# Quarter products 5 to 7 of a Strassen step in one-bank sums, two of them with 512-column matmuls, and eleven row sums a batch

## The chip, the cores and the metric

The kernel runs on one core of one Trainium2 chip. The metric is device time in microseconds (us) of one execution; lower is better. The core has engines with queues of their own that run side by side and meet at semaphores: TensorE (PE, matmuls into PSUM; its weight loads are shown as PEld), VectorE (DVE), ScalarE (ACT), GpSimd (POOL) and SyncE (SP), whose queue issues nearly all DMAs here. The kernel lays PSUM out as eight banks of 512 float32 columns on 128 partitions: two single ones (`ps_y`) and three tiles of two (`ps_u`, `ps_v`, `ps_p`).

## The reference

For each of 8 batches of 256 rows (H = 1024), an adapter matrix chosen by an index is applied, then a feed-forward layer with a routed low-rank addition, and the input is added:

```python
y = einsum('bsi,boi->bso', x, weight[adapter_ids])        # first product
logits = y @ gate_w.T + expert_bias
top1 = argmax(logits, axis=-1)                            # 4 experts
base = einsum('bth,oh->bto', y, W_up)                     # second product
z = einsum('nh,erh->ner', y, lora_A)                      # rank 8 for each expert
d = einsum('ner,ehr->neh', z, lora_B) * SCALE
out = x + base + sum over e of d[:, e] * one_hot(top1)[:, e]
```

## The kernel before, in words

All matmuls are in fp32r. Each operand is split in a high part (rounded by ScalarE) and a low part (the remainder, by VectorE), and a product is made of three matmuls: high x high, high x low, low x high. TensorE takes, for every batch b, first_product(b): eight output blocks c, each 8 pairs of a 512-column and a 256-column matmul into `ps_y[c % 2]`, which give y. Then comes the second product. Batches 0 and 1 (`b < PLAIN`) do it plainly: 512-column matmuls into one bank for each of four output quarters (`quarter`), with gates and logits apart. Batches 2 to 7 do a Strassen step with seven products (`PARTS = 7`) of quarter matrices: the left sides are A11, S1..S4 and so on, made of y by VectorE; the right sides are B11, T1..T4 and so on, made of W_up once and kept.

In the Strassen step `product(b, n, ps, p, q, ...)` makes product n of left part p and right part q, in four k steps of six matmuls (`quarter_wide`): three operand pairs, each with the 512 output columns cut in two halves of 256. Half h goes to columns 0 to 255 of bank h of a two-bank tile (`ps_u`, `ps_v` or `ps_p`). The room behind the second half, columns from 256 of bank 1, takes 72 or 36 gate and LoRA-A columns in products 1 to 4. Products 5 to 7 have no gate columns. Sums build up in PSUM: products 1, 3, 5 and 7 accumulate in `ps_u`, 2 and 6 in `ps_v`, 4 in `ps_p`, and VectorE adds the state of a tile to the output rows after some of the products (`add_row(b, t, j, ps)`: row block t, column half j, 128x512 elements, one step of `row_step` each). There are eight such sums a Strassen batch. TensorE's products wait for the sums that read a tile they go on writing.

VectorE's order is written out by hand in its `strassen(b)`: the low parts of y (`y_lo_part`), the row sums, the gate sums (`g_kept`, `g_sum`, `zg`), `choose` (expert choice, some 13 small steps that end in `z_parts`), the split of the next batch's input (`x_lo`, four steps), and of its first adapter blocks (`w_lo_part`). TensorE transposes `z_parts` in the middle of product 6 (`transpose_z`), ScalarE copies it back (`z_back`), and four LoRA sums follow (`add_lora`, `add_lora_wide`), one to each output quarter, then product 7. In batch 2 VectorE also splits the second half of T4 between two row sums (`t_lo(T4, 1)`). SyncE's queue stores a batch's rows when `row_step` has reached the last sum of each row block (`store_rows(b, 1, 7)`, `store_rows(b, 0, 8)`), and only then loads further ones.

Of the kernel before, what the change touches and what calls it, by code (L numbers as in the profile page):

```python
# [25 lines left out]
def build(nc, xT, x, ids, w, w_up, gl, lora_b, bias, out):  # L26
# [9 lines left out]
    Q = OC // 2  # L36
# [36 lines left out]
    UNITS_AFTER = range(3, UNITS)  # L73

    parts_before = [4 * min(b, PLAIN) + PARTS * max(b - PLAIN, 0) for b in range(B + 1)]
    rows_before = [4 * min(b, PLAIN) + 8 * max(b - PLAIN, 0) for b in range(B + 1)]
    sums_before = [SUMS * max(b - PLAIN, 0) for b in range(B + 1)]
    gates_before = [5 * max(b - PLAIN, 0) for b in range(B + 1)]
    products_before = [PARTS * max(b - PLAIN, 0) for b in range(B + 1)]
# [1 line left out]
    with ExitStack() as ctx:  # L81
# [70 lines left out]
        def out_cols(ps):  # L152
            return ps[:, :, 0:QUART]
# [85 lines left out]
        def _(sp):  # L239
# [35 lines left out]
            def store_rows(b, t, n):  # L275
                sp.wait_ge(row_step, rows_before[b] + n)
                sp.dma_start(out[b, t * P:(t + 1) * P, :], rows[:, t, :]).then_inc(stored[t], 16)

            def store_part(b, t, j, n):
                sp.wait_ge(row_step, rows_before[b] + n)  # L280
                part = slice(j * HALF, (j + 1) * HALF)
                sp.dma_start(out[b, t * P:(t + 1) * P, part], rows[:, t, part]).then_inc(stored[t], 16)

            def store_batch(b):
                if b < PLAIN:
                    store_rows(b, 0, 2)
                    store_rows(b, 1, 4)
                else:
                    store_rows(b, 1, 7)
                    store_rows(b, 0, 8)  # L290

            def load_blocks(first, stop, i):
                for n in range(first, min(stop, BLOCKS)):
# [23 lines left out]
            for b in range(1, B):  # L317
# [8 lines left out]
                if b + 1 < B:  # L326
                    load_x(b + 1)
                i = load_blocks(first + OC - 1, first + OC, i)
            store_rows(B - 1, 1, 7)
            store_part(B - 1, 0, 0, 7)  # L330
            store_part(B - 1, 0, 1, 8)
            sp.wait_ge(stored[0], (B + 1) * 16)
            sp.wait_ge(stored[1], B * 16)

# [165 lines left out]
        def _(dve):  # L500
            def x_lo(b, q):
                dve.wait_ge(x_hi_ready, b * XQ + q + 1)
                ks = slice(q * XK, (q + 1) * XK)
                dve.tensor_tensor(x_hilo[:, 1, ks, :], x_raw[:, 1, ks, :], x_hilo[:, 0, ks, :].bitcast(F32),  # L504
                                  ALU.subtract).then_inc(x_ready, 1)
# [183 lines left out]
            def strassen(b):  # L689
                dve.wait_ge(y_full_ready, (b + 1) * OC)  # L690
                y_add(S2, A22, S3, ALU.subtract, slice(Q - 1, Q))
                dve.wait_ge(y_sum, sums_before[b] + 3)
                y_lo_part(b, 2, S3)
                y_add(S4, A12, S2, ALU.subtract)
                y_add(S1, A21, A22, ALU.add)
                dve.wait_ge(y_sum, sums_before[b] + 5)
                y_lo_part(b, 3, S2)
                dve.wait_ge(rows_in[0], (b + 1) * 16)
                dve.wait_ge(product_done, products_before[b] + 1)
                dve.tensor_copy(g_kept[:, 0, :], gate_out(ps_u)).then_inc(g_step, 1)  # L700
                add_row(b, 0, 0, out_cols(ps_u))
                y_lo_part(b, 4, A12)
                y_lo_part(b, 5, S1)
                y_lo_part(b, 6, A22)
                y_lo_part(b, 7, S4)
                dve.wait_ge(rows_in[1], (b + 1) * 16)
                dve.wait_ge(product_done, products_before[b] + 2)
                dve.tensor_copy(g_kept[:, 1, :], gate_out(ps_v)).then_inc(g_step, 1)
                add_row(b, 1, 1, out_cols(ps_v))
                if b == PLAIN:  # L710
                    t_lo(T4, 1)
                dve.wait_ge(product_done, products_before[b] + 3)
                dve.wait_ge(g_step, gates_before[b] + 2)
                dve.tensor_tensor(g_sum[:, 1, :], gate_out(ps_u), g_kept[:, 1, :], ALU.add).then_inc(g_step, 1)
                add_row(b, 1, 0, out_cols(ps_u))
                if b + 1 < B:
                    x_lo(b + 1, 0)
                    x_lo(b + 1, 1)
                dve.wait_ge(product_done, products_before[b] + 4)
                dve.tensor_tensor(g_sum[:, 0, :], gate_out(ps_p), g_kept[:, 0, :], ALU.add).then_inc(g_step, 1)  # L720
                dve.wait_ge(g_step, gates_before[b] + 4)
                dve.tensor_tensor(zg[:, :, :], g_sum[:, :, 0:GL], g_sum[:, :, GL:2 * GL], ALU.add).then_inc(g_step, 1)
                dve.wait_ge(g_step, gates_before[b] + 5)
                choose(b, zg[:, :, :])
                if b + 1 < B:
                    x_lo(b + 1, 2)
                    x_lo(b + 1, 3)
                dve.wait_ge(product_done, products_before[b] + 5)
                add_row(b, 1, 1, out_cols(ps_u), after=2)
                for n in splits_after(b):  # L730
                    w_lo_part(n)
                lora_before = PLAIN * 4 + (b - PLAIN) * 4
                dve.wait_ge(out_done, lora_before + 1)
                add_row(b, 1, 1, ps_y[1][:, :].rearrange("p (h n) -> p h n", h=2), after=4)
                dve.wait_ge(out_done, lora_before + 2)
                add_row(b, 0, 0, out_cols(ps_p), after=1)
                dve.wait_ge(out_done, lora_before + 3)
                add_row(b, 1, 0, out_cols(ps_v), after=3)
                dve.wait_ge(out_done, lora_before + 4)
                dve.wait_ge(product_done, products_before[b] + 7)  # L740
                add_row(b, 0, 1, out_cols(ps_u))

            dve.memset(warm_f[:, :], 0.0).then_inc(warm_step, 1)
            dve.wait_ge(warm_step, 1)
# [18 lines left out]
        def _(pe):  # L763
# [117 lines left out]
                        add_lora(b, 1, 0, ps_plain[1, 0])  # L881
                add_lora(b, 1, 1, ps_plain[1, 1])

            def product(b, n, ps, p, q, start, stop=False):
                for k in range(Q):
                    last = quarter_wide(ps, p, q, k, start and k == 0, stop and k == Q - 1, n in (1, 2, 3, 4))
                    if n == 6 and k == 1:
                        transpose_z(b)
                last.then_inc(product_done, 1)

            def strassen(b):
# [17 lines left out]
                pe.wait_ge(y_ready, y_before + 4)  # L909
                product(b, 4, ps_p, A12, B21, True)  # L910
                pe.wait_ge(y_ready, y_before + 5)
                pe.wait_ge(row_step, rows_done + 3)
                product(b, 5, ps_u, S1, T1, False)
                if first:
                    pe.wait_ge(t_ready, t_count(T4, 1))
                pe.wait_ge(row_step, rows_done + 2)
                pe.wait_ge(y_ready, y_before + 6)
                product(b, 6, ps_v, A22, T4, False)
                pe.wait_ge(zt_ready, b * T + 2)
                add_lora(b, 1, 1, ps_y[1][:, :], True)  # L920
                add_lora_wide(b, 0, 0, ps_p)
                add_lora_wide(b, 1, 0, ps_v)
                pe.wait_ge(row_step, rows_done + 4)
                add_lora_wide(b, 0, 1, ps_u)
                pe.wait_ge(y_ready, y_before + 7)
                product(b, 7, ps_u, S4, B22, False, True)

            warm_up()
            for b in range(B):
# [41 lines left out]
```

## Time and profile before

| | |
|---|---|
| median of 3 runs | 374.62 us (374.54 to 375.24) |
| the profiled execution | 374.81 us |
| its span, first to last instruction | 373.0 us |
| TensorE busy | 367.5 us, 99%, 2348 matmuls |
| VectorE busy | 262.4 us, 70% |
| ScalarE busy | 159.4 us, 43% |
| DMA, both ways | 68.19 MB, mean 183 GB/s |

The profile is of one execution. Its engines' busy times overlap, so they don't add up to the span. A matmul's duration in a row (0.28 us for 256 columns, 0.39 for 512) is from start to the modelled end, while the next one starts before that; what a matmul costs the stream is read from one start to the next. In the same way a VectorE row of 0.69 us gives way to the next after 0.60. In the chain of waits a piece such as "x24" is 24 matmuls in a row, and its time is what the whole piece took. Batches are counted from 0; a Strassen batch lasts 44.1 us, of which 21.9 are its Strassen step.

### The profile page before, as it was taken

How to read it: one execution, taken by the hardware profiler on the slowest of the kernel's cores; microseconds unless marked ns; L12 is line 12 of the kernel's file. 1: busy time of each engine (PE TensorE's matmuls, PEld its weight loads, DVE VectorE, ACT ScalarE, POOL GpSimd, SP SyncE). 2: the span in 40 equal slices, each digit the busy share in tenths (PEclk: the TensorE clock that was granted, in tenths of full speed). 3: DMA queues.
4: the chain of work that ended last, by engine and by line, in shares of the span. 5: the costliest groups of instructions: out<-in, count | busy, mean ns of one | idle time of the engine just before them, and what ended most of it. 6: DMA issues, size and time to landing. Idle time of an engine off the chain costs nothing.

```text
span 373.0 us, 6260 instructions
## 1 busy us (share of the span) xinstructions
PE 367.5 (99%) x2348; PEld 334.7 (90%) x2348; DVE 262.4 (70%) x519; ACT 159.4 (43%) x320; POOL 6.6 (2%) x18
## 2 busy tenths in 40 slices
PE   7999999999999999999999999999999999999996
PEld 5888888888888999889998899989999899988996
DVE  4777587696758988678755786567874777746752
ACT  5667363642527543465115651155513553144300
POOL 1000500000000000000000000000000000000000
PEclk9999999999999999999999999999999999999999
DMA  7999975871069730687026760376404861160002
GB/s 244 402 394 312 408 286 182 325 226 57 0 192 340 252 119 0 226 302 243 21 96 210 270 216 3 147 250 231 163 2 178 324 213 76 49 234 0 2 1 114
DMA packets 19598, 68.19 MB, mean 183 GB/s; under 512 B 2288, under 2 KB 2416, under 8 KB 19568
## 3 DMA queue, kind: packets, MB, share of 16 engines
q1 hardware_dynamic: 19280, 66.74, 50.0%
q10 hardware_dynamic: 288, 1.05, 0.8%
q8 instruction: 19, 0.31, 0.3%
q14 instruction: 11, 0.09, 0.1%
HBM read 59.39 MB, written 8.39 MB: 182 GB/s over the span
## 4 chain that ended last, share of the span: by engine, by line
PE 97%; SPq 1%; DMA 1%; DVE 0%; issue 0%; ACT 0%; DVEq 0%
PE ps_y L785 31%; PE ps_u L796 19%; PE ps_y L787 16%; PE ps_v L796 10%; PE ps_p L796 5%; PE ps_u L803 2%; PE ps_v L803 2%; PE ps_u L807 2%; PE ps_v L805 2%; PE ps_u L805 2%; PE ps_v L807 2%; PE ps_p L816 1%; DMA w_raw<-w_dram 1%; SPq L241 1%; PE ps_p L847 0%; PE ps_v L847 0%
## 5 line engine op out<-in xcount | busy, mean ns | idle before, releaser
L785 PE MATMUL ps_y<-x_hilo,w_hi 128*128 128x512 f32 x512 | 178.3, 392 | 0.3 <-DVE w_lo L510 0.3
L787 PE MATMUL ps_y<-x_hilo,w_lo 128*128 128x256 f32 x512 | 143.2, 280 | 0.0
L785 PEld LDWEIGHTS ps_y<-x_hilo,w_hi 128*128 128x128 f32 x512 | 95.8, 187 | 22.1 <-DVE w_lo L510 0.8
L787 PEld LDWEIGHTS ps_y<-x_hilo,w_lo 128*128 128x128 f32 x512 | 96.7, 189 | 0.1
L517 DVE TENSOR_TENSOR w_lo<-w_raw,w_hi 128x512 fp32r<-128x512 f32 x126 | 81.3, 688 | 16.9 <-ACT w_hi L376 16.2
L376 ACT CAST w_hi<-w_raw 128x512 fp32r<-128x512 f32 x126 | 71.8, 624 | 3.4 <-DMA w_raw<-w_dram 3.3
L391 ACT COPY small<-ps_y 128x256 f32<-128x256 f32 x64 | 23.8, 372 | 107.2 <-PE ps_y L787 107.0
L562 DVE TENSOR_TENSOR y_raw<-ps_y,small 128x256 f32<-128x256 f32 x64 | 27.2, 425 | 47.1 <-ACT small L391 47.1
L796 PE MATMUL ps_u<-up_lo,y_parts 128*128 128x256 f32 x192 | 38.4, 281 | 0.0
L796 PE MATMUL ps_u<-wide_hi,y_parts 128*128 128x256 f32 x192 | 34.8, 293 | 0.0
L573 DVE TENSOR_TENSOR y_parts<-y_raw,y_parts 128x512 fp32r<-128x512 f32 x50 | 32.5, 687 | 1.3 <-ACT y_parts L394 0.9
L394 ACT CAST y_parts<-y_raw 128x512 fp32r<-128x512 f32 x50 | 28.8, 619 | 9.6 <-DVE y_raw L568 9.6
L796 PE MATMUL ps_u<-thin_hi,y_parts 128*128 128x256 f32 x192 | 32.8, 283 | 0.0
L796 PEld LDWEIGHTS ps_u<-up_lo,y_parts 128*128 128x128 f32 x192 | 31.1, 189 | 0.0
L408 ACT CAST zT<-ps_y 128x128 fp32r<-128x128 f32 x16 | 3.5, 269 | 63.8 <-PE ps_y L835 63.8
L796 PEld LDWEIGHTS ps_u<-wide_hi,y_parts 128*128 128x128 f32 x192 | 27.5, 188 | 0.2
L796 PEld LDWEIGHTS ps_u<-thin_hi,y_parts 128*128 128x128 f32 x192 | 27.3, 190 | 0.0
L580 DVE TENSOR_TENSOR rows<-ps_u,rows 128x512 f32<-128x512 f32 x28 | 19.0, 684 | 7.3 <-PE ps_u L796 7.2
L504 DVE TENSOR_TENSOR x_hilo<-x_raw,x_hilo 128x512 fp32r<-128x512 f32 x32 | 20.5, 685 | 3.6 <-ACT x_hilo L363 3.4
L363 ACT CAST x_hilo<-x_raw 128x512 fp32r<-128x512 f32 x32 | 17.9, 617 | 3.5 <-DMA x_raw<-xT_dram 3.1
L796 PE MATMUL ps_v<-up_lo,y_parts 128*128 128x256 f32 x96 | 19.2, 282 | 0.0
L796 PE MATMUL ps_v<-thin_hi,y_parts 128*128 128x256 f32 x96 | 17.6, 286 | 0.0
(108 smaller groups left out, 393.7 us busy)
## 6 DMA issues: line engine op xcount, KB each, us to landing
w_raw<-w_dram SPq DMA_DIRECT2D x64, 512.0 KB, 4.4
rows<-x_dram SPq DMA_DIRECT2D x16, 512.0 KB, 5.7
out_dram<-rows SPq DMA_DIRECT2D x15, 512.0 KB, 2.6
x_raw<-xT_dram SPq DMA_DIRECT2D x14, 512.0 KB, 5.0
up_raw<-w_up_dram SPq DMA_DIRECT2D x8, 512.0 KB, 12.4
wide_stage<-w_up_dram SPq DMA_DIRECT2D x4, 512.0 KB, 14.0
thin_stage<-w_up_dram SPq DMA_DIRECT2D x4, 512.0 KB, 9.4
x_raw<-xT_dram ACTq DMA_DIRECT2D x2, 512.0 KB, 4.2
```

Of the source, the lines that this page charges most:

```text
L363: act.copy(x_hilo[:, 0, ks, :], x_raw[:, 1, ks, :]).then_inc(x_hi_ready, 1)
L376: act.copy(w_hi[:, n % RING, part], w_raw[:, n % RAWS, part]).then_inc(w_hi_ready, QUARTERS // HALVES)
L391: act.copy(small[:, c % 2, :], ps_y[c % 2][:, S:2 * S]).then_inc(y_small_ready, 1)
L394: act.copy(y_parts[:, p, :, 0, :], y_raw[:, p, :, 1, :]).then_inc(y_hi_ready, 1)
L504: dve.tensor_tensor(x_hilo[:, 1, ks, :], x_raw[:, 1, ks, :], x_hilo[:, 0, ks, :].bitcast(F32), ALU.subtract).then_inc(x_ready, 1)
L517: dve.tensor_tensor(w_lo[:, n % RAWS, part], w_raw[:, n % RAWS, part], w_hi[:, n % RING, part].bitcast(F32), ALU.subtract).then_inc(w_read ...
L562: dve.tensor_tensor(y_raw[:, p:p + 2, c % Q, 1, :], ps_y[c % 2][:, 0:S].rearrange("p (t n) -> p t n", t=T), small[:, c % 2, :].rearrange(" ...
L573: dve.tensor_tensor(y_parts[:, p, :, 1, :], y_raw[:, p, :, 1, :], y_parts[:, p, :, 0, :].bitcast(F32), ALU.subtract).then_inc(y_ready, 1)
L580: dve.tensor_tensor(rows[:, t, part].rearrange("p (h n) -> p h n", h=2), ps, rows[:, t, part].rearrange("p (h n) -> p h n", h=2), ALU.add) ...
L785: pe.matmul(ps_y[c % 2][:, :], w_hi[:, n % RING, cols], x_hilo[:, :, k, :], start=(k == 0), stop=False)
L787: last = pe.matmul(ps_y[c % 2][:, S:2 * S], w_lo[:, n % RAWS, cols], x_hilo[:, 0, k, :], start=False, stop=(k == KC - 1))
L796: last = pe.matmul(ps[:, h, 0:end - h * QUART], y_parts[:, p, k, y, :], up_lo[:, q, k, cols] if up is None else up(q, k, cols), start=star ...
```

## The change

Products 5, 6 and 7 no longer use both banks of their tile. Product 5 starts a sum of its own in bank 0 of `ps_u`, product 6 in bank 0 of `ps_v`; both through a new `product_thin`, which is built on `quarter`: three 512-column matmuls for each k. Product 7 accumulates upon product 5 in bank 0 of `ps_u`, through a new `product_halves` that keeps six 256-column matmuls for each k, in the order of before, both halves in one bank. Since products 5 and 6 don't accumulate upon what their tiles held, three more row sums bring that to the output: `ps_v` after product 2 is added to (1, 0) too, `ps_u` after product 3 to (1, 1) and (0, 1) too. The LoRA sums to (1, 0) and (0, 1) are one 512-column matmul each. The counts in waits and stores follow: product 5 waits for the sixth row sum of the batch (before: the third), product 6 for the third (before: the second), the LoRA sum to (0, 1) for the seventh (before: the fourth).

```diff
-    rows_before = [4 * min(b, PLAIN) + 8 * max(b - PLAIN, 0) for b in range(B + 1)]
+    rows_before = [4 * min(b, PLAIN) + 11 * max(b - PLAIN, 0) for b in range(B + 1)]
@@ SyncE
-                    store_rows(b, 1, 7)
-                    store_rows(b, 0, 8)
+                    store_rows(b, 1, 10)
+                    store_rows(b, 0, 11)
@@ VectorE, strassen(b)
                 add_row(b, 1, 1, out_cols(ps_v))
+                add_row(b, 1, 0, out_cols(ps_v))
                 if b == PLAIN:
                     t_lo(T4, 1)
...
-                add_row(b, 1, 0, out_cols(ps_u))
+                add_row(b, 1, 0, out_cols(ps_u), after=3)
+                add_row(b, 1, 1, out_cols(ps_u), after=2)
+                add_row(b, 0, 1, out_cols(ps_u))
                 if b + 1 < B:
                     x_lo(b + 1, 0)
-                    x_lo(b + 1, 1)
...
                 choose(b, zg[:, :, :])
                 if b + 1 < B:
+                    x_lo(b + 1, 1)
+                dve.wait_ge(product_done, products_before[b] + 5)
+                add_row(b, 1, 1, ps_u[:, 0, :].rearrange("p (h n) -> p h n", h=2), after=5)
+                if b + 1 < B:
                     x_lo(b + 1, 2)
                     x_lo(b + 1, 3)
-                dve.wait_ge(product_done, products_before[b] + 5)
-                add_row(b, 1, 1, out_cols(ps_u), after=2)
...
-                add_row(b, 1, 0, out_cols(ps_v), after=3)
+                add_row(b, 1, 0, ps_v[:, 0, :].rearrange("p (h n) -> p h n", h=2), after=4)
...
-                add_row(b, 0, 1, out_cols(ps_u))
+                add_row(b, 0, 1, ps_u[:, 0, :].rearrange("p (h n) -> p h n", h=2), after=6)
@@ TensorE
+            def product_thin(b, n, ps, p, q, start):
+                for k in range(Q):
+                    last = quarter(ps, p, q, k, start and k == 0, False)
                     if n == 6 and k == 1:
                         transpose_z(b)
+                last.then_inc(product_done, 1)
+
+            def product_halves(b, ps, p, q):
+                for k in range(Q):
+                    for n, (y, up) in enumerate(((0, up_hi), (0, None), (1, up_hi))):
+                        for h in range(2):
+                            cols = slice(h * QUART, (h + 1) * QUART)
+                            last = pe.matmul(ps[:, cols], y_parts[:, p, k, y, :],
+                                             up_lo[:, q, k, cols] if up is None else up(q, k, cols),
+                                             start=False, stop=k == Q - 1 and n == 2, skip_group_check=True)
                 last.then_inc(product_done, 1)
...
-                pe.wait_ge(row_step, rows_done + 3)
-                product(b, 5, ps_u, S1, T1, False)
+                pe.wait_ge(row_step, rows_done + 6)
+                product_thin(b, 5, ps_u[:, 0, :], S1, T1, True)
...
-                product(b, 6, ps_v, A22, T4, False)
+                product_thin(b, 6, ps_v[:, 0, :], A22, T4, True)
...
-                add_lora_wide(b, 1, 0, ps_v)
-                pe.wait_ge(row_step, rows_done + 4)
-                add_lora_wide(b, 0, 1, ps_u)
+                add_lora(b, 1, 0, ps_v[:, 0, :])
+                pe.wait_ge(row_step, rows_done + 7)
+                add_lora(b, 0, 1, ps_u[:, 0, :])
                 pe.wait_ge(y_ready, y_before + 7)
-                product(b, 7, ps_u, S4, B22, False, True)
+                product_halves(b, ps_u[:, 0, :], S4, B22)
```

How the instructions stand in a row, at three places of batch 3. First VectorE between products 2 and 4, before (L708 and L714 are gate sums behind products 2 and 3, L580 is a row sum, L504 is x_lo, L720 the gate sum behind product 4):

```order
L708 COPY g_kept<-ps_v 128x72 [waits product_done,rows_in1]
L580 TENSOR_TENSOR rows<-ps_v,rows 128x512
L714 TENSOR_TENSOR g_sum<-ps_u,g_kept 128x72 [waits g_step,product_done]
L580 TENSOR_TENSOR rows<-ps_u,rows 128x512
L504 TENSOR_TENSOR x_hilo<-x_raw,x_hilo 128x512 [waits x_hi_ready] x2
L720 TENSOR_TENSOR g_sum<-ps_p,g_kept 128x72 [waits product_done]
```

and now (L715 and L722 are the gate sums, two lines moved):

```order
L708 COPY g_kept<-ps_v 128x72 [waits product_done,rows_in1]
L580 TENSOR_TENSOR rows<-ps_v,rows 128x512 x2
L715 TENSOR_TENSOR g_sum<-ps_u,g_kept 128x72 [waits g_step,product_done]
L580 TENSOR_TENSOR rows<-ps_u,rows 128x512 [waits row_step] x2
L580 TENSOR_TENSOR rows<-ps_u,rows 128x512
L504 TENSOR_TENSOR x_hilo<-x_raw,x_hilo 128x512 [waits x_hi_ready]
L722 TENSOR_TENSOR g_sum<-ps_p,g_kept 128x72 [waits product_done]
```

Three row sums have come in, one ahead of the gate sum of product 3 and two behind it, and one of two x_lo steps has left.

VectorE again, from the end of the expert choice (L626) to the first LoRA row sum (from ps_y), before:

```order
L626 TENSOR_TENSOR z_parts<-zm,z_parts 128x2x32 [waits z_step]
L626 TENSOR_TENSOR z_parts<-zm,z_parts 128x2x32
L504 TENSOR_TENSOR x_hilo<-x_raw,x_hilo 128x512 [waits x_hi_ready] x2
L580 TENSOR_TENSOR rows<-ps_u,rows 128x512 [waits row_step,product_done]
L517 TENSOR_TENSOR w_lo<-w_raw,w_hi 128x512 [waits w_hi_ready] x2
L580 TENSOR_TENSOR rows<-ps_y,rows 128x512 [waits row_step,out_done]
```

and now:

```order
L626 TENSOR_TENSOR z_parts<-zm,z_parts 128x2x32 [waits z_step]
L626 TENSOR_TENSOR z_parts<-zm,z_parts 128x2x32
L504 TENSOR_TENSOR x_hilo<-x_raw,x_hilo 128x512 [waits x_hi_ready]
L580 TENSOR_TENSOR rows<-ps_u,rows 128x512 [waits row_step,product_done]
L504 TENSOR_TENSOR x_hilo<-x_raw,x_hilo 128x512 [waits x_hi_ready] x2
L517 TENSOR_TENSOR w_lo<-w_raw,w_hi 128x512 [waits w_hi_ready] x2
L580 TENSOR_TENSOR rows<-ps_y,rows 128x512 [waits row_step,out_done]
```

The row sum that reads product 5 now stands after one x_lo step and ahead of two, where it stood behind both of two.

TensorE from the end of product 6 over the LoRA sums to the start of product 7, before (L796 is quarter_wide, L840 and L847 are LoRA sums):

```order
L796 MATMUL ps_v<-thin_hi,y_parts 128x256 x4
L796 MATMUL ps_v<-up_lo,y_parts 128x256 x2
L796 MATMUL ps_v<-thin_hi,y_parts 128x256 x2
L840 MATMUL ps_y<-lb_parts,zT 128x512 [waits zt_ready]
L847 MATMUL ps_p<-lb_parts,zT 128x256 [waits zt_ready]
L847 MATMUL ps_p<-lb_parts,zT 128x256
L847 MATMUL ps_v<-lb_parts,zT 128x256 [waits zt_ready]
L847 MATMUL ps_v<-lb_parts,zT 128x256
L847 MATMUL ps_u<-lb_parts,zT 128x256 [waits zt_ready,row_step]
L847 MATMUL ps_u<-lb_parts,zT 128x256
L796 MATMUL ps_u<-thin_hi,y_parts 128x256 [waits y_ready]
```

and now (L807, L809 and L811 are quarter, L844 and L851 LoRA sums, L905 is product_halves):

```order
L807 MATMUL ps_v<-thin_hi,y_parts 128x512
L809 MATMUL ps_v<-up_lo,y_parts 128x512
L811 MATMUL ps_v<-thin_hi,y_parts 128x512
L844 MATMUL ps_y<-lb_parts,zT 128x512 [waits zt_ready]
L851 MATMUL ps_p<-lb_parts,zT 128x256 [waits zt_ready]
L851 MATMUL ps_p<-lb_parts,zT 128x256
L844 MATMUL ps_v<-lb_parts,zT 128x512 [waits zt_ready]
L844 MATMUL ps_u<-lb_parts,zT 128x512 [waits zt_ready,row_step]
L905 MATMUL ps_u<-thin_hi,y_parts 128x256 [waits y_ready]
```

The halves of product 6 and of two LoRA sums have become single 512-column matmuls; the LoRA sum to ps_p and the first matmuls of product 7 have kept 256 columns.

## Rows read from the trace of the kernel before

**Rows 1.** The page, parts 1 and 2: busy time, and granted clock in 40 slices.
```profile
PE 367.5 (99%) x2348; PEld 334.7 (90%) x2348; DVE 262.4 (70%) x519; ACT 159.4 (43%) x320; POOL 6.6 (2%) x18
...
PEclk9999999999999999999999999999999999999999
```

**Rows 2.** The page, part 4: chain that ended last, shares by engine.
```profile
PE 97%; SPq 1%; DMA 1%; DVE 0%; issue 0%; ACT 0%; DVEq 0%
```

**Rows 3.** List of waits, a wait of TensorE: total us, times, longest.
```profile
PE ps_y L785 <- DVE w_lo L510: 0.3, 1, 0.3
```

**Rows 4.** Chain of waits in batch 3: start us, us, engine, tile, line, count.
```profile
183.53 2.87 PE ps_u L796 x24
186.40 1.44 PE ps_v L796 x12
187.83 0.17 PE ps_y L835 x2
188.00 1.48 PE ps_v L796 x12
...
190.20 0.24 PE ps_u L847 x2
190.44 2.88 PE ps_u L796 x24
193.32 0.23 PE ps_y L785
193.55 0.12 PE ps_y L787
```

**Rows 5.** TensorE in time, batches 1 and 4: start us, us, instruction.
```profile
96.60 0.39 PE L807 MATMUL ps_u<-wide_hi,y_parts 128*128 128x512 f32 x1
...
98.22 0.39 PE L803 MATMUL ps_v<-thin_hi,y_parts 128*128 128x512 f32 x1
...
100.97 0.33 PE L835 MATMUL ps_y<-eye,z_parts 128*128 128x128 f32 x2
...
101.42 0.40 PE L805 MATMUL ps_v<-up_lo,y_parts 128*128 128x512 f32 x1
...
102.59 0.63 PE L840 MATMUL ps_u<-lb_parts,zT 128*128 128x512 f32 x2
...
193.16 0.40 PE L785 MATMUL ps_y<-x_hilo,w_hi 128*128 128x512 f32 x1
```

**Rows 6.** TensorE in time, the gates of batch 1.
```profile
91.72 2.03 PE L816 MATMUL ps_p<-y_parts,wide_hi 128*72 128x256 f32 x16
93.59 0.40 PE L803 MATMUL ps_u<-wide_hi,y_parts 128*128 128x512 f32 x1
```

**Rows 7.** VectorE in time, batch 3, products 3 to 6.
```profile
180.53 0.23 DVE L714 TENSOR_TENSOR g_sum<-ps_u,g_kept 128x72 f32<-128x72 f32 x1 [1.40 <-PE ps_u L796]
180.68 0.68 DVE L580 TENSOR_TENSOR rows<-ps_u,rows 128x512 f32<-128x512 f32 x1
181.27 1.28 DVE L504 TENSOR_TENSOR x_hilo<-x_raw,x_hilo 128x512 fp32r<-128x512 f32 x2
183.57 0.23 DVE L720 TENSOR_TENSOR g_sum<-ps_p,g_kept 128x72 f32<-128x72 f32 x1 [1.01 <-PE ps_p L796]
...
186.24 1.29 DVE L504 TENSOR_TENSOR x_hilo<-x_raw,x_hilo 128x512 fp32r<-128x512 f32 x2
187.44 0.68 DVE L580 TENSOR_TENSOR rows<-ps_u,rows 128x512 f32<-128x512 f32 x1
188.99 1.29 DVE L517 TENSOR_TENSOR w_lo<-w_raw,w_hi 128x512 fp32r<-128x512 f32 x2 [0.86 <-ACT w_hi L376]
```

**Rows 8.** VectorE in time, batch 2.
```profile
134.92 1.22 DVE L551 TENSOR_TENSOR up_lo<-up_raw,thin_hi 128x1024 fp32r<-128x1024 f32 x1
136.41 0.23 DVE L714 TENSOR_TENSOR g_sum<-ps_u,g_kept 128x72 f32<-128x72 f32 x1 [0.27 <-PE ps_u L796]
...
139.45 0.23 DVE L720 TENSOR_TENSOR g_sum<-ps_p,g_kept 128x72 f32<-128x72 f32 x1 [1.01 <-PE ps_p L796]
```

More of the change, by code:

```diff
@@ L328, in _ @@
                 i = load_blocks(first + OC - 1, first + OC, i)
-            store_rows(B - 1, 1, 7)
-            store_part(B - 1, 0, 0, 7)
-            store_part(B - 1, 0, 1, 8)
+            store_rows(B - 1, 1, 10)
+            store_part(B - 1, 0, 0, 10)
+            store_part(B - 1, 0, 1, 11)
             sp.wait_ge(stored[0], (B + 1) * 16)
@@ L733, in strassen @@
                 dve.wait_ge(out_done, lora_before + 1)
-                add_row(b, 1, 1, ps_y[1][:, :].rearrange("p (h n) -> p h n", h=2), after=4)
+                add_row(b, 1, 1, ps_y[1][:, :].rearrange("p (h n) -> p h n", h=2), after=7)
                 dve.wait_ge(out_done, lora_before + 2)
@@ L882, in plain, with product @@
                 add_lora(b, 1, 1, ps_plain[1, 1])
-            def product(b, n, ps, p, q, start, stop=False):
+            def product(b, n, ps, p, q, start):
                 for k in range(Q):
-                    last = quarter_wide(ps, p, q, k, start and k == 0, stop and k == Q - 1, n in (1, 2, 3, 4))
+                    last = quarter_wide(ps, p, q, k, start and k == 0, False, True)
+                last.then_inc(product_done, 1)
+            def product_thin(b, n, ps, p, q, start):
+                for k in range(Q):
+                    last = quarter(ps, p, q, k, start and k == 0, False)
                     if n == 6 and k == 1:
                         transpose_z(b)
+                last.then_inc(product_done, 1)
+            def product_halves(b, ps, p, q):
[6 more added lines that the diff above has]
+                                             start=False, stop=k == Q - 1 and n == 2, skip_group_check=True)
                 last.then_inc(product_done, 1)
@@ L911, in strassen @@
                 pe.wait_ge(y_ready, y_before + 5)
-                pe.wait_ge(row_step, rows_done + 3)
-                product(b, 5, ps_u, S1, T1, False)
+                pe.wait_ge(row_step, rows_done + 6)
+                product_thin(b, 5, ps_u[:, 0, :], S1, T1, True)
                 if first:
                     pe.wait_ge(t_ready, t_count(T4, 1))
-                pe.wait_ge(row_step, rows_done + 2)
+                pe.wait_ge(row_step, rows_done + 3)
                 pe.wait_ge(y_ready, y_before + 6)
-                product(b, 6, ps_v, A22, T4, False)
+                product_thin(b, 6, ps_v[:, 0, :], A22, T4, True)
                 pe.wait_ge(zt_ready, b * T + 2)
```

## The prediction

> **What bounds the kernel now.** I read four views in this order. The page's first parts show TensorE busy for 367.5 of 373.0 us, with a digit of 9 (the highest) for the granted clock in all forty slices, so at 2.4 GHz [rows 1]. The chain that ended last goes through TensorE for 97% of the span [rows 2]. The list of waits has only one wait of TensorE for another engine after its warm-up that is worth a row, 0.3 us at the very start [rows 3]. So TensorE never stands still once it has begun, and what ends last everywhere in batches 2 to 7 (counted from 0) is its own stream. A change is worth exactly what it takes from the stream or what waits it brings into it. The chain through batch 3 shows the pieces that the change touches: product 5 in 2.87 us, product 6 in 1.44 + 1.48 us around two transposes, the LoRA sums, product 7 in 2.88 us [rows 4].
>
> **The width of the matmuls (products 5 and 6).** Each product streams 4 x 3 x 512 = 6144 columns. Before they go as 24 matmuls of 256 columns, after as 12 of 512. The columns stay the same, the number of starts halves. Product 5 takes 2.87 us / 24 = 0.1196 us a matmul, 0.239 us for 512 columns [rows 4]. What a 512-column matmul with the same kind of operands takes is seen in batch 1, which multiplies the same way in one bank: twelve from 98.22 to 100.97 us are 2.75 us, 0.229 each; seven from 96.60 to 98.22 give 0.231; five from 101.42 to 102.59 give 0.234 [rows 5]. I take 0.231: twelve are 2.77 us, 0.10 us less than 2.87. Product 6 keeps its transposes and gains nearly the same: 2.92 us without them goes to 2.77 if the slow restart behind the transposes were also gone, but in batch 1 that restart is there too (from the transposes at 100.97 to 101.42, 0.45 us for two transposes and one 512-column matmul) [rows 5], so I take 0.09. Ends: with 0.234, 2.81 us, 0.06 less in each product, 0.12 a batch; with 0.229, 2.75 us, 0.12 less in each, 0.24 a batch.
>
> **The LoRA sums.** Two of three wide ones, for (1,0) and (0,1), become one 512-column matmul each: 0.24 us a pair [rows 4] to 0.231, 0.01 each, 0.02 a batch. The third, into ps_p, stays.
>
> **Product 7** keeps 24 matmuls of 256 columns, but both halves now go into one bank, where they alternated between two. No row has just this. Nearest rows: the gates of batch 1, sixteen 256-column matmuls all into one bank, start at 91.72 and the next line starts at 93.59: 1.87 us, 0.117 each [rows 6]; and the first product, where a 512-column matmul and a 256-column one write the same bank in turn in 0.23 + 0.12 us [rows 4]. One bank shows no penalty there. Ends: 24 x 0.117 = 2.81, 0.07 less; and, as 2.88 / 24 = 0.120 is already what it has, 0.06 more as a cautious end (as much as the width is worth at its low end). I take nothing.
>
> **Three more row sums on VectorE.** Each takes a slot of 0.60 us (180.68 to 181.27) [rows 7], 1.8 us a batch, 10.8 us in six batches, and none of it stands in the chain if it fits into its idle time. Step by step in batch 3. The first extra sum, (1,0) from ps_v, falls in the 1.40 us that VectorE idles ahead of 180.53: it starts when that idle time began, at 179.1, and ends by 179.8. Then, after product 3: the gate sum at 180.53, and now three sums from ps_u at 180.68, 181.27 and 181.87; the third has ended by 182.56. Product 5 must now wait for the sixth row sum, since it clears the bank that these three read. Its first matmul stands at 183.53 in the chain, and the chain's times are 0.16 us behind the engine's own record (193.32 against 193.16 for the same matmul) [rows 4, 5], so it starts at 183.37: a margin of 0.8 us. One x_lo step (half of the 1.29 us pair) still fits ahead of the gate sum at 183.57; it would end at 183.1. The choice of the expert then runs as before, up to 186.24. The second x_lo step goes there, the sum that reads product 5 at 186.84 instead of 187.44, the other two x_lo steps behind it until 188.7, still ahead of 188.99, when the w_lo steps get their input [rows 7]. The next batch's first product, which needs x_lo, comes at 193.16. All four x_lo steps therefore keep over 4 us of margin. Queued behind the waiting product 5 is everything on TensorE; a wait there would be paid in full.
>
> In batch 2 there is one thing more: the split of T4 at 134.92, which stands between the sums and takes until 136.41 less 0.27 idle, so 1.22 us. Pushed back by one sum of 0.60, it ends at 136.74, and the gate sum that started at 136.41 starts up to 0.33 late. The sixth sum then ends at 136.74 + 0.15 + 0.59 + 0.60 + 0.69 = 138.8. Product 5 starts 0.20 ahead of the gate sum at 139.45 (as 183.37 against 183.57), at 139.25 [rows 8]. Margin 0.45 us, the smallest of all. I put the price at nothing.
>
> The LoRA sum for (0,1) now waits for the seventh row sum; it ends at 187.5, and that LoRA sum comes at 190.20 in the chain [rows 4]. SyncE's queue keeps its order; its stores wait for the tenth and eleventh sum in place of the seventh and eighth, which are the same last sums. The tail behind product 7 (one sum, a store) is the same.
>
> **Sum.** 0.10 + 0.09 + 0.02 = 0.21 us a batch, six batches: 1.2 us. The profiled execution took 374.81 us (span 373.0 and 1.8 around it): 373.6 after. The median of the runs is 0.19 below the profiled one, so 373.4, a gain of 0.33%. The low ends together (0.12 + 0.01 - 0.06 = 0.07 a batch) give 0.4 us, 374.2; the high ends (0.24 + 0.02 + 0.07 = 0.33) give 2.0 us, 372.6.
>
> **Rivals.** A, the width is worth next to nothing: the 256-column matmul of the gates took 0.117 us, so two of them 0.234, against 0.231 for one of 512 [rows 5, 6]. If 0.117 is the true price of 256 columns and the 0.1196 of product 5 has another source that stays (its operands, its traffic), then 26 pairs a batch save 0.003 us each: 0.08 a batch, 0.5 us, 374.1. Against it: product 7, product 5 and the LoRA pairs all show 0.12, with different operands.
> The Trainium skill, TensorE: Matmul & The Clock Gate, section Back-to-back issue gap, speaks on this side: at full clock the gap of a matmul is its columns divided by 2.4 GHz plus about 2.5 ns, whatever its width. By that rule an estimate of 26 x 6 x 2.5 ns = 0.4 us would be saved, 374.2. The trace disagrees in the size: 256 columns take 0.120 us here, not the 0.109 of the rule, and 512 take 0.231, not 0.216.
>
> B, slower: the sixth row sum is late and product 5 waits for it. The place is the stretch between product 3 and product 5. It decides from 0.8 us of delay (0.45 in batch 2), and makes the kernel slower than before from 0.8 + 0.21 = 1.0. That would need the three sums to take 1.0 us more than their 1.8, as if reading ps_u while TensorE writes ps_p slowed them to 0.95 each. If they took 1.2 each, the sixth would end at 180.68 + 3.6 = 184.3, a stall of 0.9 a batch less 0.21: six times 0.7, 378.8. Against it: the sum at 180.68 reads ps_u just then, and takes 0.60 [rows 7].
>
> C, one bank makes product 7 faster too: 0.07 a batch more, or 512 columns at 0.229: 1.6 to 2.0 us in all, 372.6 to 373.0.
>
> D, the change does what it says but other engines' shifts eat it: the w_lo steps and the splits behind the sums come later by the three sums (1.8 us a batch) and touch the next first product. Below 0.2 us a batch would be lost: about 374.6. VectorE idles 1.40 + 1.01 + 0.86 us in this stretch alone [rows 7].
>
> **Numbers.** Forecast (1.0 to 1.5 us, 373.1 to 373.6) 0.60; C 0.14; A 0.12; D 0.07; B 0.07. No change can be told from what is within 0.2%, 0.75 us. The forecast and C are faster, 0.74, and a part of A, 0.02: 0.76. A and D give 0.16 to the same, B and a piece of D the rest, 0.08. The range runs from 372.7 to 374.2: it holds the forecast, most of C and A.
>
> **What would show it.** In the profile after: product 5 as twelve matmuls in 2.77 us in the chain, product 6 with 1.39 us on each side of the transposes; product 7 at 2.88; no row of waits of TensorE for row sums; VectorE's three sums from ps_u ending about 0.8 us ahead of product 5; busy time of VectorE up by some 11 us; 512-column LoRA sums at 0.23. I am wrong if product 5 stays above 2.83 us (A), if a gap opens ahead of product 5 (B), or ahead of the next first product (D).

## The result: slower by 0.15%, and the profile after

The changed kernel takes 375.66 us (median of 19 runs, 375.28 to 376.12); the kernel before, in 19 runs beside it, 375.14 (374.54 to 376.38). The ratio is 1.0015, 95% interval 1.0009 to 1.0021: slower, by 0.5 us, where 1.2 us less was forecast. That is less than the 0.2% within which the prediction calls two kernels the same, but the interval leaves out 1. The profiled execution took 375.46 us with a span of 373.7, 0.7 more than the span before.

The page of the changed kernel, the parts that answer to [rows 1, 2]:

```profile
span 373.7 us, 5966 instructions
PE 367.6 (98%) x2192; PEld 326.9 (87%) x2192; DVE 272.7 (73%) x537; ACT 159.3 (43%) x320; POOL 6.6 (2%) x18
PEclk9999999999999999999999999999999999999999
PE 96%; SPq 1%; DMA 1%; issue 1%; DVE 0%; ACT 0%
```

156 matmuls are gone, the clock is the same, and TensorE is as busy as it was. VectorE has its 10 us more. TensorE's own instructions in time through batch 3 show the Strassen step (it answers to [rows 4]):

```profile
183.55 0.40 PE L807 MATMUL ps_u<-thin_hi,y_parts 128*128 128x512 f32 x1
...
186.31 0.39 PE L807 MATMUL ps_v<-thin_hi,y_parts 128*128 128x512 f32 x1
...
187.68 0.33 PE L839 MATMUL ps_y<-eye,z_parts 128*128 128x128 f32 x2
...
189.29 0.39 PE L844 MATMUL ps_y<-lb_parts,zT 128*128 128x512 f32 x1
...
190.23 0.40 PE L905 MATMUL ps_u<-thin_hi,y_parts 128*128 128x256 f32 x2
```

Product 5 takes 186.31 - 183.55 = 2.76 us (2.87 before), product 6 with its transposes 2.98 (3.09 before), product 7 from 190.23 to the next first product at 193.10 2.87 (2.89 before, read the same way). All this is as forecast. The margins are too. This is VectorE, after product 3 of batches 2 and 3, in time:

```profile
136.66 0.22 DVE L715 TENSOR_TENSOR g_sum<-ps_u,g_kept 128x72 f32<-128x72 f32 x1
136.80 1.87 DVE L580 TENSOR_TENSOR rows<-ps_u,rows 128x512 f32<-128x512 f32 x3
...
180.71 0.23 DVE L715 TENSOR_TENSOR g_sum<-ps_u,g_kept 128x72 f32<-128x72 f32 x1 [0.81 <-PE ps_u L800]
180.86 1.87 DVE L580 TENSOR_TENSOR rows<-ps_u,rows 128x512 f32<-128x512 f32 x3
```

The sixth sum ends at 182.73, 0.8 us ahead of product 5 at 183.55, in batch 2 at 138.67, 0.6 ahead of 139.25. TensorE waits for none of them.

The time went into the part that the change does not touch, the first product. It is a row of 64 pairs, each a 512-column and a 256-column matmul; the pitch of a pair is the time from its start to the start of the next. Here is the first product of batch 3, from its first matmul to the first of the Strassen step, in the kernel before and in the one after:

```profile
149.03 0.40 PE L785 MATMUL ps_y<-x_hilo,w_hi 128*128 128x512 f32 x1
...
171.23 0.43 PE L796 MATMUL ps_u<-wide_hi,y_parts 128*128 128x256 f32 x2
```

```profile
148.80 0.40 PE L789 MATMUL ps_y<-x_hilo,w_hi 128*128 128x512 f32 x1
...
171.41 0.44 PE L800 MATMUL ps_u<-wide_hi,y_parts 128*128 128x256 f32 x2
```

The same 64 pairs, with nothing between them and no wait, take 22.20 us before and 22.61 after: 0.347 and 0.353 a pair. Nearly all of the difference is in the slot of the 512-column matmul, from its start to the next start: 0.230 us before, 0.236 on average after, where that of the 256-column one is 0.117 in both. The same two stretches by windows, before and after (length, busy time and count of PE, PEld, DVE, ACT and POOL, granted clock, DMA share, GB/s):

```profile
149.03:171.23 22.20, 22.20 (x130) 19.56 (x129) 15.37 (x28) 10.91 (x23) 0.00 (x0) 1.00 0.72 256
148.80:171.41 22.61, 22.61 (x131) 19.60 (x130) 15.64 (x28) 10.92 (x23) 0.00 (x0) 1.00 0.71 255
```

The granted clock is 1.00, full speed, in both, TensorE is busy throughout, and the DMAs and ScalarE do the same. So neither the clock nor the traffic of the DMAs tells the two apart. Looked at one by one, at the start of batch 4, before and after:

```profile
193.51 0.40 PE L785 MATMUL ps_y<-x_hilo,w_hi 128*128 128x512 f32 x1
...
193.86 0.39 PE L785 MATMUL ps_y<-x_hilo,w_hi 128*128 128x512 f32 x1
...
194.21 0.39 PE L785 MATMUL ps_y<-x_hilo,w_hi 128*128 128x512 f32 x1
...
194.55 0.39 PE L785 MATMUL ps_y<-x_hilo,w_hi 128*128 128x512 f32 x1
```

```profile
193.45 0.40 PE L789 MATMUL ps_y<-x_hilo,w_hi 128*128 128x512 f32 x1
...
193.81 0.40 PE L789 MATMUL ps_y<-x_hilo,w_hi 128*128 128x512 f32 x1
...
194.16 0.40 PE L789 MATMUL ps_y<-x_hilo,w_hi 128*128 128x512 f32 x1
...
194.51 0.40 PE L789 MATMUL ps_y<-x_hilo,w_hi 128*128 128x512 f32 x1
```

Starts of pairs before are 0.35, 0.35, 0.34 apart and go on at 0.347 through the whole first product. After, they are 0.36, 0.35, 0.35 apart, a pattern of three pairs that repeats 21 times. It is there in batches 3 to 7, each first product that follows a changed Strassen step; batches 1 and 2, which follow plain ones, stay at 0.347 in both kernels. The account: 5 x 0.41 = 2.05 us are lost, and six Strassen steps of 21.69 (193.10 - 171.41) in place of 21.93 win 6 x 0.24 = 1.44. That is 0.6 us lost in all, and the spans differ by 0.65 (373.7 against 373.0).

### The profile page after: what moved, and what is told of

Read it like the earlier page. It is cut to its first block, busy times and chain, and to the rows that moved or that the text cites. A ratio compares the mean times of both kernels' runs of the same rounds, so it can differ in the third digit from the quotient of the medians.

```text
span 373.7 us, 5966 instructions
## 1 busy us (share of the span) xinstructions
PE 367.6 (98%) x2192; PEld 326.9 (87%) x2192; DVE 272.7 (73%) x537; ACT 159.3 (43%) x320; POOL 6.6 (2%) x18
## 4 chain that ended last, share of the span: by engine, by line
PE 96%; SPq 1%; DMA 1%; issue 1%; DVE 0%; ACT 0%
PE ps_y L789 32%; PE ps_y L791 16%; PE ps_u L800 10%; PE ps_p L800 5%; PE ps_v L800 5%; PE ps_u L905 4%; PE ps_v L807 4%; PE ps_u L807 4%; PE ps_u L809 3%; PE ps_v L811 3%; PE ps_v L809 3%; PE ps_u L811 3%; PE ps_p L820 1%; DMA w_raw<-w_dram 1%; SPq L241 1%; PE ps_u L844 1%
## 5 line engine op out<-in xcount | busy, mean ns | idle before, releaser
L789 PE MATMUL ps_y<-x_hilo,w_hi 128*128 128x512 f32 x512 | 180.2, 396 | 0.9 <-DVE w_lo L510 0.9
L580 DVE TENSOR_TENSOR rows<-ps_u,rows 128x512 f32<-128x512 f32 x40 | 26.1, 682 | 6.9 <-issue 6.8
L504 DVE TENSOR_TENSOR x_hilo<-x_raw,x_hilo 128x512 fp32r<-128x512 f32 x32 | 20.8, 684 | 3.8 <-ACT x_hilo L363 3.5
L809 PE MATMUL ps_u<-up_lo,y_parts 128*128 128x512 f32 x56 | 22.0, 394 | 0.0
L809 PE MATMUL ps_v<-up_lo,y_parts 128*128 128x512 f32 x56 | 22.0, 392 | 0.0
L800 PE MATMUL ps_u<-up_lo,y_parts 128*128 128x256 f32 x96 | 19.1, 280 | 0.0
L800 PE MATMUL ps_v<-wide_hi,y_parts 128*128 128x256 f32 x96 | 17.5, 294 | 0.0
L800 PE MATMUL ps_p<-wide_hi,y_parts 128*128 128x256 f32 x96 | 17.5, 294 | 0.0
L568 DVE TENSOR_TENSOR y_raw<-y_raw 128x512 f32<-128x512 f32 (+2 forms) x30 | 16.9, 580 | 0.4
```

What stands on the lines that cost most here:

```text
L580: dve.tensor_tensor(rows[:, t, part].rearrange("p (h n) -> p h n", h=2), ps, rows[:, t, part].rearrange("p (h n) -> p h n", h=2), ALU.add) ...
L789: pe.matmul(ps_y[c % 2][:, :], w_hi[:, n % RING, cols], x_hilo[:, :, k, :], start=(k == 0), stop=False)
L800: last = pe.matmul(ps[:, h, 0:end - h * QUART], y_parts[:, p, k, y, :], up_lo[:, q, k, cols] if up is None else up(q, k, cols), start=star ...
L809: pe.matmul(ps, y_parts[:, p, k, 0, :], up_lo[:, q, k, :], start=False, stop=False, skip_group_check=True)
```

## The experiments

Three theories were set against one another. T1: TensorE's stream runs in one of several repeating patterns of starts, and which one the first product falls into is set by the matmuls right ahead of it, here called the entry. It later became P: what counts is the offset in time with which the first product enters, so any odd matmul ahead can change the pattern. T2: VectorE's three more sums disturb it. T3: the 512-column products 5 and 6 lead to it. K came later: the PSUM bank written last decides, with `ps_y` counted as banks 0 and 1 and `ps_u` as 2 and 3. Times are medians, ratios those to the kernel before, run beside each. Kernels were run in different groups, in which the kernel before had medians from 374.98 to 375.16, so a difference between two groups can be off by some 0.2 us.

**Product 7 in 512 columns too.**

```diff
-                product_halves(b, ps_u[:, 0, :], S4, B22)
+                product_thin(b, 7, ps_u[:, 0, :], S4, B22, False)
```

> The changed kernel, with product 7 as twelve matmuls of 512 columns too. Three theories of why the first product's pair of matmuls (512 and 256 columns) takes 0.353 us from batch 3 on where it took 0.347. T1, pattern of starts: what TensorE runs right before the first product (product 7 as 256-column matmuls in one bank) leads its stream into a slower repeating pattern. T2, VectorE: the three more row sums disturb it. T3: products 5 and 6 in 512 columns lead into it. T1: with 512-column matmuls ahead, as in the plain batches 0 and 1, pairs go back to 0.347; product 7 takes 2.78: 375.7 - 5 x 0.41 - 6 x 0.09 = about 373.1. T2 and T3: pairs stay at 0.353, only product 7 gets shorter: about 375.1.

Measured: 374.75, ratio 0.999 (0.998 to 0.9999). Pairs stayed at 0.353 (first product of batch 3 from 148.74 to 171.34). The gain is product 7's alone, which takes 2.72 us in place of 2.86. It fits T2 and T3, and T1's forecast, that 512-column matmuls ahead give the fast pattern, is missed.

**Products 5 and 6 in 256-column halves, one bank.**

```diff
-                product_thin(b, 5, ps_u[:, 0, :], S1, T1, True)
+                product_halves(b, 5, ps_u[:, 0, :], S1, T1, True)
...
-                product_thin(b, 6, ps_v[:, 0, :], A22, T4, True)
+                product_halves(b, 6, ps_v[:, 0, :], A22, T4, True)
...
-                product_halves(b, ps_u[:, 0, :], S4, B22)
+                product_halves(b, 7, ps_u[:, 0, :], S4, B22, False)
```

> The changed kernel with products 5 and 6 in 256-column matmuls again, both halves in one bank as in product 7; sums, waits and LoRA matmuls stay. It undoes the width alone. T1: product 7 is still one-bank 256, pairs stay at 0.353; six batches lose 0.2 each: about 376.9. T3: pairs go back to 0.347: 375.7 + 1.2 - 2.1 = 374.8. T2: as T1, 376.9.

Measured: 376.79, ratio 1.004 (1.0026 to 1.0054), pairs at 0.353. T3 falls: the slow pattern is there without any 512-column product. The width of products 5 and 6 is worth 376.79 - 375.66 = 1.1 us between the medians (1.3 between the spans of 374.9 and 373.7), as forecast.

**All sums and waits of the change, TensorE's matmuls as before.** The LoRA sums are wide again, and the row sums read both banks.

```diff
-                product_thin(b, 5, ps_u[:, 0, :], S1, T1, True)
+                product(b, 5, ps_u, S1, T1, True)
...
-                product_thin(b, 6, ps_v[:, 0, :], A22, T4, True)
+                product(b, 6, ps_v, A22, T4, True)
...
-                product_halves(b, ps_u[:, 0, :], S4, B22)
+                product(b, 7, ps_u, S4, B22, False)
```

> Eleven row sums, waits and order of VectorE as in the changed kernel, but TensorE's matmuls all as before: 256 columns in two banks for products 5 to 7, wide LoRA sums. Only the sums and waits are new. T1 and T3: pairs at 0.347, same as before: 375.1. T2: pairs at 0.353 from batch 3 on, 5 x 0.41 more: 377.2.

Measured: 374.85, ratio 0.9996 (0.9986 to 1.0006), pairs at 0.347 (149.09 to 171.29). T2 falls: eleven sums cost nothing. Between this run and the last the sums and waits are the same in number and order. What differs is TensorE's stream, and with it the banks that three sums read.

**A 128-column matmul more, behind product 7 of the changed kernel, and of the kernel before.** Both add the same lines there:

```diff
+                pe.matmul(ps_y[0][:, 0:P], zT[:, 0, :], lb_parts[:, 0:P], start=True, stop=True,
+                          skip_group_check=True)
```

> The changed kernel with one more matmul of 128 columns between product 7 and the next first product (its result is overwritten and used by nobody). T1: a pattern of starts can be tipped by one odd matmul: pairs at 0.347 in the batches behind it, 375.7 - 2.05 + 6 x 0.06 = 374.0; if the slow pattern is where the first product always ends up after 256-column matmuls, it stays at 0.353 and 376.0. T2, T3: 376.0.

> The kernel before, with one more 128-column matmul into bank 0 between product 7 and the next first product (result unused). P, phase: which repeating pattern the first product falls into hangs on the offset at which its first matmul enters, and any odd matmul ahead can shift it: pairs may go from 0.347 to 0.353 here, though nothing else is changed: 375.0 + 5 x 0.41 + 6 x 0.06 = 377.4. K, bank: the slow pattern follows when the last matmul ahead wrote an even bank (bank 0 here): also 0.353. If neither holds, pairs stay at 0.347, 375.4.

Measured: in the changed kernel 376.32, ratio 1.003 (1.0019 to 1.004), pairs at 0.353: the added matmul does not bring the fast pattern back. In the kernel before 375.62, ratio 1.0017 (1.0008 to 1.0027). Its first product of batch 3, in time:

```profile
149.53 0.45 PE L785 MATMUL ps_y<-x_hilo,w_hi 128*128 128x512 f32 x1
...
149.93 0.39 PE L785 MATMUL ps_y<-x_hilo,w_hi 128*128 128x512 f32 x1
...
150.28 0.40 PE L785 MATMUL ps_y<-x_hilo,w_hi 128*128 128x512 f32 x1
...
150.63 0.39 PE L785 MATMUL ps_y<-x_hilo,w_hi 128*128 128x512 f32 x1
...
150.97 0.40 PE L785 MATMUL ps_y<-x_hilo,w_hi 128*128 128x512 f32 x1
...
151.32 0.39 PE L785 MATMUL ps_y<-x_hilo,w_hi 128*128 128x512 f32 x1
...
171.77 0.43 PE L796 MATMUL ps_u<-wide_hi,y_parts 128*128 128x256 f32 x2
```

The first pair takes 0.40 us. The 63 behind it take 171.77 - 149.93 = 21.84 us, 0.347 each, but in a rhythm of their own, 0.350 and 0.343 by turns, which no other kernel has in these batches. So one matmul ahead changed the rhythm and left the mean pitch as it was. The forecasts of 0.353, K's after bank 0 and P's as one that may come, are missed; the third one, 0.347 and 375.4, is met but for the long first pair, 0.05 us a batch. The changed kernel has that long first pair too (22.66 us for the 64, where it had 22.61).

**Products 5 and 7 in bank 3 in place of bank 2,** in the changed kernel and with 512 columns throughout, and the 128-column matmul of the changed kernel into bank 3. The first edit moves product 5, the LoRA sum to (0,1) and two row sums in the same way; its last line:

```diff
...
-                product_halves(b, ps_u[:, 0, :], S4, B22)
+                product_halves(b, ps_u[:, 1, :], S4, B22)
```

> The changed kernel with products 5 and 7 and their LoRA sum in the second bank of ps_u in place of the first (TensorE's last bank ahead of the first product is then 3, as in the kernel before, in place of 2). Same widths, counts and waits. K: pairs go back to 0.347, 375.7 - 2.05 = 373.6. P: the offsets are the same as in the changed kernel, pairs stay at 0.353, 375.7.

> The changed kernel with one more 128-column matmul ahead of each next first product, as in the run before with bank 0, but into bank 3. K: pairs at 0.347, 374.0. P: as with bank 0, 0.353 and 376.3.

> Products 5, 6 and 7 all in 512 columns, products 5 and 7 in the second bank of ps_u. K: pairs at 0.347, 374.75 - 2.05 = 372.7. P: 0.353 as with the first bank, 374.75.

Measured: 375.53 (1.0003 to 1.0021), 376.27 (1.002 to 1.0044), 374.77 (0.9981 to 0.9999). Each is within 0.15 us of its twin in the other bank, pairs at 0.353. K falls.

**The LoRA sum to (0,1) behind product 7,** with 512 columns throughout and in the changed kernel. Against the kernel with 512 columns throughout it is:

```diff
-                add_lora(b, 0, 1, ps_u[:, 0, :])
                 pe.wait_ge(y_ready, y_before + 7)
                 product_thin(b, 7, ps_u[:, 0, :], S4, B22, False)
+                add_lora(b, 0, 1, ps_u[:, 0, :])
```

> Products 5, 6 and 7 in 512 columns, one bank, and the LoRA sum to (0,1) behind product 7 in place of ahead of it. TensorE then ends the batch as the plain batches 0 and 1 end (512-column matmuls of products, last a 512-column LoRA sum), after which the first product runs at 0.347. P (the pattern hangs on the offset at entry, set by the matmuls just ahead): pairs go back to 0.347: 374.75 - 2.05 = 372.7. If the pattern is set by something else that came with the change, they stay at 0.353: 374.75.

> The changed kernel with its LoRA sum to (0,1), 512 columns, behind product 7 (256 columns, one bank). P: the entry is a new one, either pattern is possible: 373.6 with pairs at 0.347, 375.6 at 0.353.

Measured: 374.87 (0.9989 to 1.0007) and 375.74 (1.0005 to 1.0024), pairs at 0.353 in both. A miss for P in the form in which I put it: to end with the kinds of matmuls that a plain batch ends with isn't enough. The second of the two had no forecast that could fail, since either pitch was allowed.

**A 256-column matmul more in the changed kernel.** The lines are as above, with `0:2 * P`.

> The changed kernel with one more matmul of 256 columns (result unused) ahead of each next first product. P: another shift of the entry; 375.6 - 2.05 + 6 x 0.12 = 374.3 if it tips to 0.347, 376.3 if it stays at 0.353.

Measured: 374.26, ratio 0.9984 (0.9975 to 0.9993). The kernel does one matmul more a batch and is 1.4 us faster than without it. TensorE in time at the start of batch 4 (L946 is the added matmul):

```profile
192.67 0.28 PE L946 MATMUL ps_y<-lb_parts,zT 128*128 128x256 f32 x1
192.79 0.40 PE L789 MATMUL ps_y<-x_hilo,w_hi 128*128 128x512 f32 x1
193.02 0.28 PE L791 MATMUL ps_y<-x_hilo,w_lo 128*128 128x256 f32 x1
193.14 0.39 PE L789 MATMUL ps_y<-x_hilo,w_hi 128*128 128x512 f32 x1
...
193.49 0.39 PE L789 MATMUL ps_y<-x_hilo,w_hi 128*128 128x512 f32 x1
...
193.83 0.39 PE L789 MATMUL ps_y<-x_hilo,w_hi 128*128 128x512 f32 x1
```

Pairs are 0.35, 0.35, 0.34 apart again, and 0.347 in batch 3 too (148.80 to 170.99, 22.19). This is the closest comparison of all: this kernel and the changed one with the 128-column matmul differ in the columns of that one matmul and in nothing else. Their instructions are the same in number and order, and so are the waits, the banks and the tiles; one runs its pairs at 0.347, the other at 0.353. Neither the count of instructions nor a wait can be what selects.

**Products 5 and 6 of the change, product 7 of the kernel before.**

```diff
-    rows_before = [4 * min(b, PLAIN) + 11 * max(b - PLAIN, 0) for b in range(B + 1)]
+    rows_before = [4 * min(b, PLAIN) + 12 * max(b - PLAIN, 0) for b in range(B + 1)]
...
                 add_row(b, 1, 1, ps_u[:, 0, :].rearrange("p (h n) -> p h n", h=2), after=5)
+                add_row(b, 0, 1, ps_u[:, 0, :].rearrange("p (h n) -> p h n", h=2), after=6)
...
-                add_lora(b, 0, 1, ps_u[:, 0, :])
+                add_lora_wide(b, 0, 1, ps_u, True)
...
-                product_halves(b, ps_u[:, 0, :], S4, B22)
+                product(b, 7, ps_u, S4, B22, False)
```

> Products 5 and 6 in one bank and 512 columns as in the changed kernel, but product 7 as in the kernel before (256 columns, halves in two banks in turn), with its LoRA sum wide and starting that tile anew; product 5 is brought to (0,1) by a twelfth row sum. P, in the form that the stream of product 7 right ahead sets the entry: pairs at 0.347 as in the two kernels that had this product 7: 375.1 - 1.4 = 373.7, faster than both. If the 512-column products 5 and 6 lead to the slow pattern by themselves: 0.353, 375.8.

Measured: 373.71, ratio 0.9963 (0.995 to 0.9977). It is the gain that was forecast for the change (374.98 - 373.71 = 1.3 us, against the kernel before beside it), got by leaving product 7 and its LoRA sum as they were, at the price of a twelfth row sum. The first product of batch 3, and product 7 and the entry of batch 4:

```profile
148.86 0.40 PE L790 MATMUL ps_y<-x_hilo,w_hi 128*128 128x512 f32 x1
...
171.06 0.43 PE L801 MATMUL ps_u<-wide_hi,y_parts 128*128 128x256 f32 x2
...
189.88 0.40 PE L801 MATMUL ps_u<-thin_hi,y_parts 128*128 128x256 f32 x2
...
192.76 0.40 PE L790 MATMUL ps_y<-x_hilo,w_hi 128*128 128x512 f32 x1
```

22.20 us for the 64 pairs, as in the kernel before; a Strassen step of 192.76 - 171.06 = 21.70, as in the changed one.

**Switched off and on elsewhere.** The 256-column matmul behind an all-512 product 7; and a 512-column or 256-column one in the kernel before (`0:4 * P`, `0:2 * P`), which has nothing else of the change.

> Products 5, 6 and 7 in 512 columns, one bank, and one more matmul of 256 columns (result unused) ahead of each next first product. P: if that matmul tips the stream as it did behind the 256-column product 7, pairs run at 0.347: 374.75 - 2.05 + 6 x 0.12 = 373.4; if the tip worked only for that entry, 0.353 and 375.5.

> The kernel before with one more matmul of 512 columns (result unused) ahead of each next first product. P says that the slow pattern has nothing to do with the change's own parts and can come up in the kernel before as well, if the entry is shifted so: with 0.347, 375.0 + 6 x 0.23 = 376.4; with 0.353, 378.5.

> The kernel before with one more matmul of 256 columns ahead of each next first product. P: another shift; with 0.347, 375.7; with 0.353, 377.8. If no shift of the kernel before ever gives 0.353 the slow pattern needs something of the change.

Measured: the first 373.53, ratio 0.9954 (0.9941 to 0.9968), pairs at 0.347 (150.44 to 172.64): the lowest time of all, with an interval that overlaps that of the kernel above, and like it faster than both the kernel before and the changed one. The two in the kernel before took 378.46, ratio 1.0084 (1.0069 to 1.0099), and 378.31, ratio 1.0087 (1.0069 to 1.0105). The kernel before took 375.16 beside them. The added matmuls themselves cost 6 x 0.23 = 1.4 and 6 x 0.12 = 0.7 us, and the pattern 2.05: 378.6 and 377.9. The second is 0.4 above that, with four runs from 377.6 to 379.1; in its trace the first product of batch 3 takes 22.61 us too. First product of batch 3 with the 512-column one in the kernel before:

```profile
150.23 0.39 PE L785 MATMUL ps_y<-x_hilo,w_hi 128*128 128x512 f32 x1
...
172.84 0.44 PE L796 MATMUL ps_u<-wide_hi,y_parts 128*128 128x256 f32 x2
```

22.61 us, 0.353 a pair: the slow pattern in a kernel with none of the change in it. The same 256-column matmul that switches it off behind a one-bank product 7 switches it on behind a two-bank one, where one of 128 columns left the mean pitch at 0.347. T2, T3 and K have no account of it. What is shown is that TensorE's own matmuls right ahead select the pitch. That they do so by an offset in time, which is P, is only argued: P allowed either pitch in about half of the runs. Where it named one, it was right when the matmuls ahead kept their widths and number or only the bank changed, and missed in the two that changed them (product 7 in 512 columns, and the LoRA sum behind it).

## Why the prediction was wrong

**What bounds the kernel**: right. TensorE never waits from batch 1 on, before or after, and the whole difference lies in its stream.

**Width of products 5 and 6**: right. 0.10 and 0.09 forecast, 2.87 - 2.76 = 0.11 and 3.09 - 2.98 = 0.11 measured (before, product 6 ran from 186.23 to 189.32 in TensorE's records). As a whole 1.1 us for the width alone (second experiment against the change). The two LoRA sums went from 0.24 to 0.23 us each, as forecast.

**Product 7 in one bank**: right in its own time (2.87 against 2.89), wrong in that this was taken for all its effect. Rival C, that one bank makes it faster by itself, gets 0.02 us, not 0.07. The changed kernel and the one that keeps products 5 and 6 of the change with product 7 of before differ by 375.66 - 373.71 = 1.95 us, nearly the whole of the 2.1 us of slower pairs.

**Three row sums**: right. VectorE has 10.3 us more work, the margins ahead of product 5 were 0.8 and 0.6 us (0.8 and 0.45 forecast), and run alone the eleven sums measured 0.9996. Rival B is out, and so is D: nothing of VectorE's is late.

**The sum**: this is the step that failed. It counted the instructions that the change touches at their new prices and every other one at its old price ("a change is worth exactly what it takes from the stream or what waits it brings into it"). But the 640 matmuls of five later first products changed price: 0.353 a pair in place of 0.347, +2.1 us, against -1.4. No rival had it. What should have warned me stood in [rows 5]: the same 512-column matmul at 0.229, 0.231 and 0.234 in three stretches of one batch, with no wait in any. I used that spread as a range for the width, and did not ask what selects the value, nor whether the untouched 0.347 could also have another value. The other value stood in the same trace: in batch 0 the kernel before runs pairs at 0.353 (rows in the last section).

**The rule weighed**: by the Trainium skill, TensorE: Matmul & The Clock Gate, section Back-to-back issue gap, the gap at full clock is the columns divided by 2.4 GHz plus about 2.5 ns; the section calls this the gap of an isolated matmul and gives a sustained figure for 512 columns beside it. Either way one width has one value. The trace disagrees: at a granted clock of 1.00 one and the same pair has a mean pitch of 0.347 or of 0.353 us.

**The range** had its upper end at 374.2 because every term was bounded from rows of the touched parts. Rival A, which shared the side, was wrong as well: the width is worth its full 0.10 a product. A part of the distance to 375.66 is no fault of the sum: it started from 374.62, the median of three runs, where 19 runs of the same kernel beside the changed one gave 375.14. Moved by these 0.5 us the range would end at 374.7, still 1.0 us too low.

## What to carry to other kernels

In a stream of matmuls that never waits, the pitch isn't a constant of the shape: in this kernel it falls into a repeating pattern that is selected at the entry and, if nothing stops the stream, kept for the 128 matmuls of a first product. After any change of such a stream compare the pitch of the parts that were not touched, before anything else. If it has moved, try another arrangement or one more small matmul ahead of the long stretch, and measure it: here 0.12 us a batch bought 0.4, and the same matmul in another kernel cost 0.4 more.

## What the runs showed that was not expected

Batch 0 of the kernel before has the slow pattern too, with no Strassen step ahead; TensorE in time there:

```profile
11.40 0.40 PE L785 MATMUL ps_y<-x_hilo,w_hi 128*128 128x512 f32 x1
...
13.87 0.40 PE L785 MATMUL ps_y<-x_hilo,w_hi 128*128 128x512 f32 x1
...
14.80 0.40 PE L785 MATMUL ps_y<-x_hilo,w_hi 128*128 128x512 f32 x1
...
30.75 0.40 PE L785 MATMUL ps_y<-x_hilo,w_hi 128*128 128x512 f32 x1
```

From 11.40 to 13.87 there are seven pairs, 0.353 each. The next pair comes late, at 14.35, and its weight load shows 0.29 us of idle time that ended with a step of VectorE. From 14.80 to 30.75 there are 46 pairs, 0.347 each. So a short stop within a first product changed the pitch with no matmul added or taken away. In the changed kernel with its LoRA sum last the same stop in batch 0 did the reverse, from 0.347 to 0.353. The pattern of batch 0 differs among the profiled executions, though their programs are the same up to there; from batch 1 on each kernel showed one and the same pattern in all its batches of a kind. That may be part of why runs of one kernel scatter by some 0.5 us; it is only argued, not tested. A longer stop in batch 0 can be another part: the profiled execution of the kernel with the lowest median (all in 512 columns and the 256-column matmul more) took 374.88 us, 1.35 above its median, and TensorE waited there 1.12 us for a split of w at the start of its second block.

Also open is what in the engine holds the pattern, and which entries lead where. Fourteen kernels enter the first product from another end of the Strassen step than the one before: eleven ran it at 0.353 and three at 0.347. The three kernels that end the step with the product 7 of before and nothing behind it (the one before among them) all ran it at 0.347, and I could foretell only those.
